# A graph layer's step sums: one conditional store per step instead of one store per four steps

## What is computed

```
xn = layernorm(x)
weight = einsum('rb,bio->rio', w_comp, bases)            # 32 relations from 8 bases
msg    = einsum('ni,rio->nro', xn, weight)[src, rel_type] * norm
gnn    = relu(segment_sum(msg, dst, 6250))
x      = x + gnn + mix(xn)                               # mix: linear attention and a small MLP
x      = x + ffn(layernorm(x))                           # ffn: 8 experts, weighted by a softmax router
```

## Time and profile before

| | |
|---|---|
| three timed runs | 3726.64 us median, 3724.68 to 3733.71 |
| profiled execution, first to last instruction | 3625.5 us |
| profiled execution, own time | not recorded beside its span; the median is 101.1 us above the span |
| busy: TensorE, VectorE, GpSimd, ScalarE | 84%, 64%, 57%, 28% |
| DMA | 864.86 MB, mean 239 GB/s |
| granted TensorE clock, mean | 0.948 |

### The profile page before, as it was taken

How to read it: one execution, slowest core, us unless ns; L and a number is a source line. 1 busy time by engine, 2 the same in 40 slices (tenths; PEclk the granted TensorE clock), 3 DMA queues, 4 the chain that set the end, 5 groups by cost and what they waited for, 6 DMA issues and landing times.

```text
span 3625.5 us, 64856 instructions
## 1 busy us (share of the span) xinstructions
PE 3058.7 (84%) x18282; PEld 2662.0 (73%) x18282; DVE 2330.1 (64%) x6228; ACT 1013.4 (28%) x1678; POOL 2077.7 (57%) x2825
## 2 busy tenths in 40 slices
PE   0058899666889999898999989899998989999887
PEld 0047777666778888787888878788887878888765
DVE  4846566767676767667666666766666676666422
ACT  0023232100223333333232333232323323232343
POOL 0046666777776666666666666666666666666100
PEclk9769999888999999999999999999999999999999
DMA  7368888877888787788878787887877878787532
GB/s 192 125 198 281 285 287 283 249 238 231 266 262 269 242 261 246 247 253 262 255 243 259 242 251 250 255 256 245 260 235 253 252 253 253 239 264 240 177 105 78
DMA packets 647443, 864.86 MB, mean 239 GB/s; under 512 B 63831, under 2 KB 524197, under 8 KB 646816
## 3 DMA queue, kind: packets, MB, share of 16 engines
q1 hardware_dynamic: 511092, 550.00, 46.6%
q0 software_dynamic: 95776, 262.27, 24.9%
q10 hardware_dynamic: 40140, 47.81, 4.0%
HBM read 552.23 MB, written 316.84 MB: 240 GB/s over the span
## 4 chain that ended last, share of the span: by engine, by line
PE 62%; DMA 14%; issue 10%; DVE 7%; POOL 3%; SPq 2%; ACT 2%; POOLq 0%; DVEq 0%; ACTq 0%
PE PS L1760 61%; DMA steps<-normed_nodes,steps 11%; POOL steps L775 3%; DVE h_low L1056 2%; DVE steps L1367 2%; PE PS L1830 1%; DVE steps L1249 1%; SPq L425 1%; DVE feed L1056 1%; ACT feed L964 1%; DMA mixbuf<-in_x_dram 1%; ACT h_high L963 1%; DMA steps<-edge_records,colc 1%; DMA step_sums<-steps 0%; SPq L370 0%
## 5 line engine op out<-in xcount | busy, mean ns | idle before, releaser
L775 POOL DMA_INDIRECT steps<-normed_nodes,steps x1968 | 1959.4, 996 | 1045.6 <-PE PS L1760 446.6
L1367 DVE SCALAR_TENSOR_TENSOR steps<-steps,PS 128x256 f32<-128x256 f32 x1968 | 943.2, 479 | 842.6 <-PE PS L1760 790.8
L1760 PE MATMUL PS<-steps 128*128 128x128 f32 x7872 | 1191.5, 289 | 283.4 <-DMA steps<-normed_nodes,steps 124.2
L1760 PEld LDWEIGHTS PS<-steps 128*128 128x128 f32 x7872 | 1089.9, 200 | 393.2 <-issue 227.9
L1760 PE MATMUL PS<-bases_s,feed 128*128 128x256 f32 x1664 | 391.8, 379 | 1.9 <-issue 1.9
L964 ACT ACTIVATE feed<-PS,bnc 128x512 f32<-128x512 f32 x416 | 317.7, 776 | 168.2 <-PE PS L1760 165.1
L1760 PEld LDWEIGHTS PS<-bases_s,feed 128*128 128x128 f32 x1664 | 304.6, 190 | 39.3 <-issue 2.2
L1324 DVE TENSOR_TENSOR steps<-steps 128x512 f32<-128x512 f32 x495 | 329.9, 687 | 4.2
L963 ACT ACTIVATE h_high<-PS,bnc 128x512 fp32r<-128x512 f32 x208 | 161.9, 778 | 551.8 <-PE PS L1760 551.8
L1760 PE MATMUL PS<-w_one,feed 128*128 128x256 f32 (+1 forms) x1028 | 305.8, 431 | 4.4 <-issue 4.4
L1760 PE MATMUL PS<-h_high,split_in 128*128 128x512 f32 x832 | 258.1, 434 | 21.5 <-ACT feed L964 21.5
(11 more groups left out here) (214 smaller groups left out, 3090.3 us busy)
## 6 DMA issues: line engine op xcount, KB each, us to landing
step_sums<-steps SPq DMA_DIRECT2D x492, 512.0 KB
split_in<-expert_split SPq DMA_DIRECT2D x104, 1024.0 KB, 8.3
feed<-step_sums SPq DMA_DIRECT2D x416, 128.0 KB
steps<-step_types SPq DMA_DIRECT2D x126, 256.0 KB
steps<-normed_nodes,steps POOLq DMA_INDIRECT x1968
mixbuf<-mix_hidden SPq DMA_DIRECT2D x53, 256.0 KB
w_zero<-in_L_ffn_Wo_dram SPq DMA_DIRECT2D x52, 256.0 KB
w_one<-in_L_ffn_Wo_dram SPq DMA_DIRECT2D x52, 256.0 KB
```

The source lines that it names most:

```text
L775: pool.indirect_dma_start(out=ring[:, k, :], out_offset=None, in_=xnD, in_offset=bass.IndirectOffsetOnAxis(ap=idxc[:, u, k:k + 1], axis=0) ...
L1367: dve.scalar_tensor_tensor(acc[:, k % ACCR, :], acc[:, (k - 1) % ACCR, :], keepc[:, k:k + 1], PS[:, a:a + C], ALU.mult, ALU.add).then_inc( ...
L1760: return pe.matmul(o, a, b, start=start, stop=stop)
```

## The change

Each step's sum gets a store of its own, which is carried out only if the next step is of another group. For this SyncE reads five group numbers for four steps from `grow` into registers and compares neighbours. A store that is not carried out still counts on its semaphore, so the waits count four stores per quarter of the ring and iteration where they counted one.

```diff
+            gregs = [sp.alloc_register(f"group{k}") for k in range(BATCH + 1)]
 
             def keep_steps(it, k):
                 q = k // BATCH
-                wait_apart(sp, "acc_done", it * UN + k + 1 + ALEAD)
-                sp.dma_start(stepD[bass.ds(it * UN + q * BATCH, BATCH), :, :].rearrange("s p n -> p s n"),
-                             acc[:, q * BATCH:(q + 1) * BATCH, :]).then_inc(sem(f"step_out{q}"), 16)
+                s0 = it * UN + q * BATCH
+                sp.load(gregs, grow[0:1, bass.ds(s0 + 1, BATCH + 1)])
+                g = [sp.snap(r, min_val=0, max_val=DUMP) for r in gregs]
+                for j in range(BATCH):
+                    wait_apart(sp, "acc_done", s0 + j + 1 + ALEAD)
+                    sp.dma_start(stepD[bass.ds(s0 + j, 1), :, :].rearrange("s p n -> p (s n)"),
+                                 acc[:, q * BATCH + j, :], cond=(g[j] != g[j + 1]), cond_hint=False
+                                 ).then_inc(sem(f"step_out{q}"), 16)
...
             def kept(it):
                 for q in range(NB):
-                    wait_apart(sp, f"step_out{q}", DLEAD + 16 * it)
+                    wait_apart(sp, f"step_out{q}", DLEAD + 16 * BATCH * it)
...
             for q in range(NB):
-                sp.wait_ge(sem(f"step_out{q}"), DLEAD + 16 * ITERS)
+                sp.wait_ge(sem(f"step_out{q}"), DLEAD + 16 * BATCH * ITERS)
...
                     if k % BATCH == 0:
-                        dve.wait_ge(sem(f"step_out{k // BATCH}"), DLEAD + 16 * it)
+                        dve.wait_ge(sem(f"step_out{k // BATCH}"), DLEAD + 16 * BATCH * it)
```

## The result

| | before | after |
|---|---|---|
| median time, us | 3730.18 (3724.68 to 3736.23, 4 runs) | 3871.41 (3857.79 to 3878.33, 4 runs) |
| ratio, 95% interval | 1 | 1.0373 [1.0346, 1.0400] |
| span of the profiled execution | 3625.5 (of the page shown) | 3875.4 |
| data moved | 864.86 MB | 658.88 MB |

The change is 3.7% slower, 141 us. The forecast was 3720 with a range to 3745; what came is the third rival, SyncE fills up.

A forecast was written before the change was run, and what follows sets the result against it. The prediction took GpSimd's gather issue as the bound: 1 us from earlier rows plus 5 us from shorter gaps, SyncE's added work costing 0, made 6 us off 3726.6, about 3720 us; range 3698 to 3745.

The forecast's parts named there:

- the third rival: SyncE's queue: lags without end above 3.6 us a batch (light stretch) or 4.3 (long loop), up to 3960; chance 0.18.
- GpSimd's pace is the bound: GpSimd's gather issue: 61 gathers per 100 us, 3.13 us for two steps, without real waits, whatever the DMA share.
- Less traffic is worth nothing: DMA stores: 207 MB less, share down to about 0.60, earning only 1 us at the end of the steps.
- the second rival: DMA engines as the real bound: 207 MB less would save 827 us, time near 2900; chance 0.02.
- Shorter odd gaps: GpSimd's 42 longer gaps, 75 us in all, shrink with lighter traffic: 5 us gained, bounds 0 and 25.
- The four conditional stores: SyncE's queue: 0.46 us each not taken, 0.75 taken; 2.1 us for four, with waits and comparisons.
- The load: SyncE's load of five group numbers into registers per four steps: taken as 0.6 us, upper bound 1.76.
- Sum 2.7 to 2.8 us, 2.2 more than now: SyncE's queue per four steps: new load plus four waits, comparisons and stores, against about 0.6 us now.
- So 2.8 fits in both, at 77% and 84% load: SyncE's queue: room of 4.3 us a batch in the long loop, 3.6 in the stretch without memsets.
- Cost 0: SyncE's added work: its lag behind other loads is covered by VectorE's spare accumulators and early weight loads, costing no time.
- The 101 us between span and median: Whole kernel: timed median 3726.64 exceeds the profiled span 3625.5 by 101 us, taken as untouched by the change.
- 4 + 25 us below: Forecast's own lower end: bounds of the row-arrival and odd-gap terms, 4 and 25 us, given as 3705.

The follow-up runs named there:

- e11: Kernel before without GpSimd's memset in every second step: 3401.09 us, ratio 0.9369 to the kernel before.
- e4: Kernel before, storing only each fourth step's sum (128 KB, always, one plain store), the other three left out: 3739.57 us, ratio 0.9998.
- e9: The changed kernel again, unedited, against the kernel before on another chip: 3629.12 us against 3631.79, ratio 0.9988.
- e16: The changed kernel once more, unedited, against the kernel before on a further chip: 3617.94 us against 3627.27, ratio 0.9970.
- e1: The kernel before again, unedited, for a second profile: 3740.75 us against 3740.11, ratio 1.0001.
- e14: Kernel before with 80 empty instructions added on SyncE behind each store, stores and traffic untouched: ratio 1.1243 to the kernel before.
- e2: Kernel before with four stores of 128 KB, each with its own wait and always carried out, per four steps: 3756.0 us, ratio 1.0043.
- e3: Kernel before with an unused register load ahead of each store; the trace has no load in it: 3736.5 us, ratio 0.9992.
- e17: The changed kernel without GpSimd's memset in every second step: 3479.05 us, ratio 0.9572 to the kernel before.
- e18: The lean form without GpSimd's memset in every second step: 3444.41 us, ratio 0.9474 to the kernel before.
- the lean form: The changed kernel with one load of 17 words per 16 steps and one wait ahead of four conditional stores: ratios 0.9966 and 0.9979 to before.
- e15: The lean form, second of its two runs, against the kernel before: ratio 0.9979.
- e13: Kernel before with 56 empty instructions added on SyncE behind each store, stores and traffic untouched: ratio 1.0078 to the kernel before.

## Why the prediction was wrong, point by point

**GpSimd's pace is the bound: right.** Its cycle is 3.13 us in after too, and e11 gains 6.3% by taking its memset away.

**Less traffic is worth nothing: right.** e4 shows it alone (0.9998), e9 and e16 with the whole change (0.9988, 0.9970). The rule of the Trainium skill, SBUF — State Buffer, that HBM is almost always the bottleneck, by which the second rival would have held, doesn't hold for this kernel: 193 MB of 865 less changed nothing (e4). The share went to 0.57 to 0.62 in the long loop, where 0.60 was forecast. Shorter odd gaps (5 us) are within what e9 and e16 leave, 3 and 9 us; no run tells them apart.

**The four conditional stores: right in size.** About 1.5 us more had been forecast, 1.3 was measured with fixed conditions, on an undisturbed SyncE.

**The load: mis-sized.** Taken at 0.6, with 1.47 seen and set aside as a load behind a store. It costs 1.08, whatever stands before it, with some 0.7 of arithmetic beside it. On an undisturbed SyncE the change thus adds 3.07 us a batch where 2.2 was forecast. This alone wouldn't have cost anything: 2.79 + 3.07 = 5.86 fits in 6.63 (e9, e16).

**The step that failed is the price of SyncE's added work: "Sum 2.7 to 2.8 us, 2.2 more than now", and with it "So 2.8 fits in both, at 77% and 84% load" and "Cost 0".** The room itself was read about right: 2.85 us of work a batch in the prediction, 2.96 in e1, on the kind of chip that was timed. But there the change works 6.92 a batch (after), so it adds 3.96 where 2.2 was forecast: 3.07 as on an undisturbed SyncE, and 0.9 more that only the disturbed one costs. The prediction's sum would have given 2.96 + 2.2 = 5.2 of 6.63; measured are 6.92 against 6.63, full. The disturbance weighs by what is in the queue: before's 13 instructions a batch cost 0.2 us more than undisturbed, the change's 38 cost 6.92 - 5.86 = 1.06 more (instructions counted in the traces). The long loop then loses about (6.92 - 6.63) x 348 = 101 us. By the windows of the two disturbed executions: up to 3330 after has made 242 + 237 + 169 + 575 + 576 = 1799 gathers, before (e1) 239 + 257 + 180 + 603 + 601 = 1880; 81 fewer at 1.66 us each are 134 of the 145 us between the spans, 53 of the 81 in the long loop from 1330 on. The third rival (it lags without end above 4.3 us for the part that the change puts in, and the price is the surplus times 348) is how it went: that part is 6.92 - 2.96 + 0.6 = 4.6 us, inside the upper bound of 4.9, and its own sum for 4.5 us is a loss of 85 us where 141 came.

**The 101 us between span and median, "which nothing here touches", were a sign that went unread.** They were no time around the span: in e1 the execution takes 3731.84 us and its span is 3730.1. The timed runs were of the disturbed kind. Its extra time isn't SyncE's work, though. Up to 3330 before made 1942 gathers in its own page's execution and 1880 in e1; 58 of the 62 are missing from 630 to 1330, and SyncE waits for VectorE in 284 of the 400 us from 630 to 1030 in e1 (by the instructions' times).

**A slip in the range.** "4 + 25 us below" 3726.6 gives 3698, not the 3705 named as the forecast's own lower end; the final range, from 3698, isn't touched by it.

**What holds up what.** That a full SyncE queue by itself makes this loss is shown by e14; that the late loads of aggregated sums are its way to TensorE is read from the traces (469.3 us in after, 796.7 in e14, 125.5 in e9), and no run moved those loads to another queue. That the queue made the loss on the disturbed chip too rests on the sum above, on after having the same pattern as e14, and on e1 to e4, which keep room there and lose 0.4% or nothing; no run filled the plain kernel's queue on a disturbed chip.

**What stays open.** What disturbs SyncE, and with it the 0.9 us that it adds to the change. The outliers of the semaphore instructions of L346 are in all four kernels on chip A (maxima of 700 to 967 ns) and in the first comparison's after, and in none on chips B to E (at most 18 ns, but for one 316 in e17). The same five traces, and no others, have about half of the semaphore events. Beside the long ones stand others of 2 or 3 ns, where the undisturbed traces have 17 at least (4 in e18), so a single duration there is no measure of work; the argument uses only sums over many batches. In e1 GpSimd's semaphore instructions have a maximum of 43 ns, so they don't share it. On a disturbed chip the kernel before also loses in the light stretch (257 gathers from 630 to 1030 against 306 in its own page's execution) although SyncE waits there; why wasn't found. And the lean form was never run on a disturbed chip: an estimate from e15's 5.1 us and the 0.2 to 1.06 that the disturbance adds in before and in the change is 5.3 to 6.1 of 6.63, at its upper end about where e13 lost 0.8%; this is worked out, not measured.

## What to carry to other kernels

A queue's room must be read from an execution like the ones that are timed. When the span and the timed median differ by 3%, run or read a second execution before any room is counted; a gap that "nothing touches" is a missing piece of the model. Don't take a waits view as complete, either: it lists what it can attribute, and in e1 that was 386 of 554 us; hold it against the instructions' own times. Count a queue's work per loop turn against the pace of the loop, and keep a tenth free: at 5.86 of 6.63 us nothing was lost, at 6.1 0.8%, at 6.92 3.7% and at 7.55 12.4%. A conditional store isn't free where it isn't carried out: with its wait and comparison four of them cost 1.3 us more of the queue than the one large store that they took the place of, and a register load over 1 us; and traffic that nobody waits for earns nothing when it goes.

## What the hardware showed that wasn't expected

SyncE's instructions differ between executions of one program on different chips: 17/17/17 ns against 2/17/701 ns for a semaphore instruction, 2.8 against 3.0 us for a batch of before, 5.86 against 6.92 for a batch of the change, and 3627 to 3634 against 3740 us for the whole kernel before. A load of five words into registers took 1.08 us and one of 17 words 3.67 us, about 0.2 us a word between these two; the load of eight words in the earlier trace rows, 1.47, is a little under that. And one 0.12 us memset in every second step costs GpSimd 0.12 + 0.81 - 0.30 = 0.63 us with the gap it opens, and the kernel was 6.3% quicker without it.
